# A fused model kernel: two sums of the recurrence moved to ScalarE, weights loaded in an earlier block, two layers cut into pieces

## The reference

```
x = x + mamba(rnn(x))          # rnn: h = tanh(h @ Wh + x_t @ Wx + b), 128 steps
                               # mamba: h = dA*h + dB*u, y = h.C ; y*rsqrt(mean(y^2)+eps)*norm_w*silu(z) @ out_proj
x = x + ffn(gru(x))            # gru: 128 steps; ffn: 3 residual blocks
                               #   h = h + qlora(gelu(layernorm(qlora(h))))
x = x + gla(cond_logits(x))    # gated linear attention
x = x + moe(lstm(x))           # lstm: 128 steps; moe: 8 experts, top 2
```

```python
y = y * lax.rsqrt(jnp.mean(jnp.square(y), axis=-1, keepdims=True) + eps) * norm_w
y = y * _silu(z)
return jnp.einsum('btd,od->bto', y, out_proj_w)
...
y = _qlora_linear(h, qweights[i0], scales[i0], biases[i0], lora_a[i0], lora_b[i0])
y = _layernorm(y, ln_gamma[blk], ln_beta[blk])
y = jax.nn.gelu(y, approximate=False)
y = _qlora_linear(y, qweights[i1], scales[i1], biases[i1], lora_a[i1], lora_b[i1])
h = y + h
```

## Time and profile before

| | us |
|---|---|
| median of 3 runs | 6985.24 (6977.26 to 6986.25) |
| the profiled execution | 6983.42 |
| its span, first to last instruction | 6981.6 |
| PE busy | 5730.2 (82%) |
| DVE busy | 5765.9 (83%) |
| ACT busy | 4481.1 (64%) |
| POOL busy | 2712.0 (39%) |
| between 2000 and 3000 us, in the recurrence: DVE, ACT busy | 917.1, 840.7 |
| between 5742 and 5797 us, in the finish: DVE, ACT busy | 37.6, 3.6 |
| between 6126 and 6160 us, in ffn: DVE, ACT busy | 19.9, 8.8 |

### The profile page before, as it was taken

One profiled execution on the slowest core, in us unless ns is written; L12 is line 12 of the kernel. 1 busy time (PEld: TensorE's weight loads), 2 busy tenths in 40 slices (PEclk: granted clock), 3 DMA queues, 4 the chain that ended last, 5 costly groups with the idle time before them and its releaser, 6 DMA issues. The chain is left out here.

```text
span 6981.6 us, 152684 instructions
## 1 busy us (share of the span) xinstructions
PE 5730.2 (82%) x49639; PEld 3105.1 (44%) x49913; DVE 5765.9 (83%) x11628; ACT 4481.1 (64%) x9795; POOL 2712.0 (39%) x2035
## 2 busy tenths in 40 slices
PE   5888888888888888888888768888888887934989
PEld 3555555555555555555555323333333334522543
DVE  4898999999999999989999789999999994446333
ACT  6888888888888888888888744444444442323322
POOL 3222222222222222222222179999999980000000
PEclk9999999999999999999999889999999998966999
DMA  0000000000000000000000010000000000000000
GB/s 8 2 2 2 2 2 2 2 2 2 2 2 2 2 2 2 2 2 2 2 2 2 20 31 4 4 3 4 4 3 4 4 2 3 4 7 3 0 18 6
DMA packets 14195, 30.48 MB, mean 4 GB/s; under 512 B 3665, under 2 KB 11602, under 8 KB 12434
## 3 DMA queue, kind: packets, MB, share of 16 engines
q1 hardware_dynamic: 13586, 22.47, 1.2%
HBM read 15.12 MB, written 7.34 MB: 3 GB/s over the span
## 5 line engine op out<-in xcount | busy, mean ns | idle before, releaser
L423 ACT ACTIVATE rx_junk<-rx_z 128x384 bf16<-128x384 f32 x2178 | 1371.5, 636 | 0.3
L1079 POOL TENSOR_TENSOR hc<-hh,cg 128x512 f32<-128x512 f32 x1024 | 1277.0, 1267 | 80.8 <-DVE hh L1059 75.3
L1000 ACT ACTIVATE ps_m<-ps_m,aneg 128x508 f32<-128x508 f32 x1024 | 673.6, 658 | 875.9 <-DVE hh L1059 834.3
L1059 DVE TENSOR_TENSOR_SCAN hh<-ps_m,bx 128x512 f32<-128x512 f32 x1024 | 1214.0, 1209 | 13.8 <-POOL bx L1083 13.8
L511 POOL TENSOR_TENSOR rx_z<-rx_z 128x512 f32<-128x512 f32 x256 | 384.8, 1503 | 1950.0 <-ACT rh_z L441 1946.7
L964 PE MATMUL ps_m<-hc,pick 128*128 128x512 f32 x2048 | 1056.0, 599 | 9.8 <-POOL hc L1079 8.5
L648 DVE TENSOR_REDUCE rh_ends<-rh_z 128x4 f32<-128x1536 f32 x512 | 960.3, 1917 | 124.3 <-ACT rh_z L441 124.3
L517 POOL TENSOR_TENSOR rx_z<-rx_z 128x1024 f32<-128x1024 f32 x274 | 656.0, 2395 | 73.4 <-DVE rx_z L612 36.7
L338 PE MATMUL r_ps<-rx_z,negid 128*128 128x256 f32 x2192 | 530.8, 384 | 103.2 <-POOL rx_z L511 90.6
L314 PE MATMUL r_ps<-rh_z,negid 128*128 128x256 f32 x2048 | 498.5, 385 | 111.6 <-ACT r_ps L435 111.6
L342 PE MATMUL r_ps<-rx_z,negid 128*128 128x512 f32 x1096 | 506.7, 605 | 62.2 <-POOL rx_z L517 62.2
(11 more groups left out here) (393 smaller groups left out, 10662.1 us busy)
## 6 DMA issues: line engine op xcount, KB each, us to landing
rows_scratch<-pc SPq DMA_DIRECT2D x48, 128.0 KB
rows<-rows_scratch SPq DMA_DIRECT2D x128, 48.0 KB
ew<-in_e SPq DMA_DIRECT2D x3, 1024.0 KB, 7.6
rh_z<-in_x_dn SPq DMA_DIRECT2D x1, 1024.0 KB, 4.8
xcur<-in_x_dn SPq DMA_DIRECT2D x1, 1024.0 KB, 5.3
out_x<-xcur SPq DMA_DIRECT2D x1, 1024.0 KB, 3.9
...
```

The source lines that it names most:

```text
L423: e.activation(junk[:, n % JUNK], xz[i][:, :, n, 2:K2].rearrange("p c k -> p k c"), ACT.Copy, accum_out=xsum[:, i, n:n + 1]).then_inc(x_fo ...
L1000: e.activation(da[un % NDA][:, :, 1:T], ps[:, un % 2, :].rearrange("p (n t) -> p n t", n=NG4)[:, :, 1:T], ACT.Exp, scale=aneg[:, 0:1]).the ...
L1059: e.tensor_tensor_scan(hh[un % NBUF][:], da[un % NDA].rearrange("p n t -> p (n t)"), bx[un % NBUF][:], 0.0, ALU.mult, ALU.add).then_inc(sc ...
L1079: e.tensor_tensor(hc[un % NHC][:], hh[un % NBUF][:], cg[:], ALU.mult).then_inc(weighted, 1)
```

## The change

1. **rnn.** The sums of the last two sequences (14 and 15) leave DVE: its fourth reduce covers two sequences instead of four, and ACT sums the two with an instruction of the same form as `x_fold`, behind the last `rest`. The sixteen x_fold of a step are distributed anew over the places of the step (before: 2, 1, 8, 5; now, with one place more: 2, 2, 1, 4, 7). POOL's `x_even_sums` no longer waits for ACT's `rest`, only for both DVE scans of x.
2. **The finish** of the state-space layer is done in four groups of four sequences; squares are made on ACT, the scale and eps of the mean are taken into the square root.
3. **Weights** of ffn, gla, lstm and moe get tiles that live from gru on, and their 24 transfers are issued in gru's block behind its own five. The copy of h stands first in ffn.
4. **ffn** works on two halves of the rows, each with its own counters; the engines take the halves in turn.

```diff
-        FIRST, SECOND, THIRD = 2, 3, 11
+        FIRST, GAP, SECOND, THIRD = 2, 4, 5, 9
...
                     seed(t, 1)
+                    x_fold(g - 1, other, FIRST, GAP)
                     e.wait_ge(re_mm, 2 * t + 1)
                     for c in range(2):
                         rest(c)
                     signs(1)
                     nudges(1)
-                    x_fold(g - 1, other, FIRST, SECOND)
+                    x_fold(g - 1, other, GAP, SECOND)
                     e.wait_ge(re_mm, 2 * t + 2)
                     for c in range(2, NRC):
                         rest(c)
+                    e.wait_ge(ra, KA * t + A_REST[NRC - 1])
+                    for i_ in range(TAIL):
+                        n = N - TAIL + i_
+                        e.activation(rjunk[:, i_], hz[:, :, n, 2:K2].rearrange("p c k -> p k c"), ACT.Copy,
+                                     accum_out=ends[:, n:n + 1]).then_inc(tail, 1)
...
+                    e.wait_ge(x_summed, 2 * g + 2)
                     for c in range(2):
-                        e.wait_ge(ra, KA * t + A_REST[2 * c])
                         x_even_sums(g, (s + 1) % 2, c)
                         x_negdifference(g, (s + 1) % 2, c)
...
                     for c in range(NRC):
                         e.wait_ge(ra, KA * t + A_REST[c])
-                        j = tl.inc(e.tensor_reduce(ends[:, quarter(c)], fold(hz, quarter(c)), mybir.AxisListType.XY, ALU.add))
+                        n = slice(quarter(c).start, min(quarter(c).stop, N - TAIL))
+                        j = tl.inc(e.tensor_reduce(ends[:, n], fold(hz, n), mybir.AxisListType.XY, ALU.add))
                     tl.wait(j)
+                    e.wait_ge(tail, TAIL * t + TAIL)
                     if s == 0:
                         e.wait_ge(xw_cp, i + 1)
                     j = tl.inc(e.tensor_tensor(pre[:], ends[:], xwT[:, s, :], ALU.add))
...
+                    for g in range(G):
+                        for h in range(H2):
+                            e.scalar_tensor_tensor(out=four(yz[:, g, h]), in0=four(yh[:, g, h]), scalar=nw[:, h:h + 1],
+                                                   in1=group(sz[:, h, :], g), op0=ALU.mult, op1=ALU.mult).then_inc(gated, 1)
...
+                    def add(g):
+                        e.wait_ge(projected, g + 1)
+                        e.tensor_tensor(group(xcur[:], g), group(xcur[:], g), four(ps[:, 4 + g, :]), ALU.add).then_inc(added, 1)
+
+                    for g in range(G):
+                        e.wait_ge(rooted, g + 1)
+                        e.reciprocal(rs[:, g], rs[:, g]).then_inc(inverted, 1)
+                        e.wait_ge(inverted, g + 1)
+                        e.wait_ge(gated, H2 * (g + 1))
+                        e.tensor_tensor(yz[:, g], yz[:, g], rs[:, g].unsqueeze(1).to_broadcast([128, H2, NG4 * T]),
+                                        ALU.mult).then_inc(scaled, 1)
+                        if g:
+                            add(g - 1)
+                    add(G - 1)
...
+                        e.activation(sq[:, g], yh[:, g], ACT.Square).then_inc(squared, 1)
+                    e.wait_ge(ready, 2)
+                    for g in range(G):
+                        e.wait_ge(total, g + 1)
+                        e.activation(rs[:, g], ps[:, g, :], ACT.Sqrt, scale=1.0 / DI, bias=eps[:, 0:1]).then_inc(rooted, 1)
...
+def load_later_weights(e, w, later):
+    tiles, loaded = later
+    f, a, l, x = (tiles[stage] for stage in "fale")
+    for dst, src in ((f["qi"][:], w["f_q"]), (f["sc"][:], w["f_s"]), (f["la"][:], w["f_la"]), (f["lb"][:], w["f_lb"]), (f["bias"][:], w["f_bc"])):
+        e.dma_start(dst, src).then_inc(loaded["f"], 16)
...
+    for dst, src in ((x["wr"][:], w["e_r"]), (x["w1"][:], w["e_1"]), (x["w3"][:], w["e_3"]), (x["w2"][:], w["e_2"])):
+        e.dma_start(dst, src).then_inc(loaded["e"], 16)
...
+                load_later_weights(e, w, later)
...
+                def rise(b, hf):
+                    if b == 0:
+                        e.wait_ge(made, V0)
+                    else:
+                        e.wait_ge(vec[hf], b * KV)
+                    for c in CHUNKS(hf):
                         for k in range(4):
                             j = e.matmul(ps[:, c, k * D:(k + 1) * D], h[:, (4 * c + k) * 128:(4 * c + k + 1) * 128],
                                          wt[:, 2 * b, :], start=True, stop=True)
-                        j.then_inc(pe, 1)
-                    for c in range(4):
-                        e.wait_ge(act, b * KA + 3 + c)
+                        j.then_inc(pe[hf], 1)
+
+                def fall(b, hf):
+                    for i, c in enumerate(CHUNKS(hf)):
+                        e.wait_ge(act[hf], b * KA + 3 + i)
                         for k in range(4):
                             j = e.transpose(ps[:, 4 + c, k * D:(k + 1) * D], y[:, 4 * c + k, :], ident[:])
-                        j.then_inc(pe, 1)
-                    for c in range(4):
-                        e.wait_ge(act, b * KA + KA)
+                        j.then_inc(pe[hf], 1)
+                    e.wait_ge(act[hf], b * KA + KA)
+                    for c in CHUNKS(hf):
                         e.matmul(ps[:, c, :], wt[:, 2 * b + 1, :], yT[:, c * 512:(c + 1) * 512], start=True, stop=True)\
-                            .then_inc(pe, 1)
+                            .then_inc(pe[hf], 1)
+
+                rise(0, 0)
+                rise(0, 1)
+                for b in range(3):
+                    fall(b, 0)
+                    if b < 2:
+                        rise(b + 1, 0)
+                    fall(b, 1)
+                    if b < 2:
+                        rise(b + 1, 1)
...
+                    for hf in range(2):
+                        e.wait_ge(vec[hf], b * KV + 4)
+                        e.activation(sq[:, rows8(hf), :], yc[:, rows8(hf), :], ACT.Square).then_inc(act[hf], 1)
+                        e.wait_ge(vec[hf], b * KV + 6)
+                        e.activation(rs[:, rows8(hf)], rs[:, rows8(hf)], ACT.Sqrt).then_inc(act[hf], 1)
+                        e.wait_ge(vec[hf], b * KV + 10)
+                        for c in CHUNKS(hf):
+                            e.activation(y[:, 4 * c:4 * c + 4, :], yc[:, 4 * c:4 * c + 4, :], ACT.Gelu).then_inc(act[hf], 1)
+                        e.wait_ge(pe[hf], b * KPE + 4)
+                        e.activation(yT[:, cols(hf)], ps[:, 4 + 2 * hf:6 + 2 * hf, :].rearrange("p a b -> p (a b)"),
+                                     ACT.Copy).then_inc(act[hf], 1)
...
+                s.inc(e.tensor_copy(h[:], XF))
                 e.wait_ge(loaded, 16 * 8)
...
+                def norm(b, hf):
+                    s, r = track[hf], rows8(hf)
+                    bc = lambda x, k: x[:, b, :].unsqueeze(1).to_broadcast([128, k, D])
+                    per = lambda x: x[:, r].unsqueeze(2).to_broadcast([128, 8, D])
+                    for i, c in enumerate(CHUNKS(hf)):
+                        e.wait_ge(pe[hf], b * KPE + i + 1)
+                        s.inc(e.tensor_tensor(yc[:, 4 * c:4 * c + 4, :], ps[:, c, :].rearrange("p (k d) -> p k d", k=4), bc(brow, 4), ALU.add))
                     s.sync()
+                    s.inc(e.tensor_reduce(mu[:, r], yc[:, r, :], AXX, ALU.add))
                     s.sync()
+                    s.inc(e.scalar_tensor_tensor(out=yc[:, r, :], in0=per(mu), scalar=-1.0 / D, in1=yc[:, r, :], op0=ALU.mult, op1=ALU.add))
+                    e.wait_ge(act[hf], b * KA + 1)
+                    s.inc(e.tensor_reduce(rs[:, r], sq[:, r, :], AXX, ALU.add))
                     s.sync()
+                    s.inc(e.tensor_scalar(rs[:, r], rs[:, r], 1.0 / D, 1e-5, ALU.mult, ALU.add))
+                    e.wait_ge(act[hf], b * KA + 2)
+                    s.inc(e.reciprocal(mu[:, r], rs[:, r]))
                     s.sync()
+                    s.inc(e.tensor_tensor(yc[:, r, :], yc[:, r, :], per(mu), ALU.mult))
                     s.sync()
+                    s.inc(e.tensor_tensor(yc[:, r, :], yc[:, r, :], bc(gam, 8), ALU.mult))
                     s.sync()
+                    s.inc(e.tensor_tensor(yc[:, r, :], yc[:, r, :], bc(bet, 8), ALU.add))
+
+                def residual(b, hf):
+                    s = track[hf]
+                    for i, c in enumerate(CHUNKS(hf)):
+                        e.wait_ge(pe[hf], b * KPE + 5 + i)
                         hc = h[:, c * 512:(c + 1) * 512]
                         s.inc(e.scalar_tensor_tensor(out=hc, in0=ps[:, c, :], scalar=bias[:, 2 * b + 1:2 * b + 2], in1=hc,
                                                      op0=ALU.add, op1=ALU.add))
                     s.sync()
+
+                for b in range(3):
+                    norm(b, 0)
+                    if b:
+                        residual(b - 1, 1)
+                    norm(b, 1)
+                    residual(b, 0)
+                residual(2, 1)
+                for hf in range(2):
```

(23 more changed lines are left out.)

183 lines of the change are left out of this document (68 added, 115 removed).

## The result

The changed kernel takes **6889.77 us** (median of 4 runs, 6885.62 to 6891.72) against 6985.74 for the kernel before on the same chip: ratio 0.9864, 95% interval 0.9848 to 0.9880. That is 1.4% faster, 96 us, where 169 were forecast (6816, range 6788 to 6866). Each part of the change does what it was built for and the sign is right; more than two thirds of the biggest term is missing.

The account below looks back on a forecast made before the run. The prediction saw a chain in every stage, not a full engine, as the bound. Recurrence 106, finish 20, loads 28, warm start 3 and halves 12 sum to 169 us off, 6816 us, own range 6793 to 6838, overall 6788 to 6866.

Parts of the forecast that it names:

- The recurrence: Recurrence loop: each of 128 steps 0.83 us shorter, 106 us in all, bounds 70 to 118.
- The shortened reduce: Recurrence step: DVE's fourth reduce covers two sequences instead of four and saves 0.87 us a step.
- holder of the product of h: Recurrence step: x_copy allows L289 at 2023.15, DVE's tanh chain wants it at 2023.46, a cover of 0.3 us.
- The new wait of `pre` for `tail`: Recurrence step: ACT's new sums end about 2012.0, the shortened reduce at 2012.95, so this wait costs nothing.
- Rival A: Recurrence: L289 waits for x_copy, the step gains 0.5 us, 64 us instead of 106; 6858 us, chance 0.12.
- B: Recurrence: the shortened reduce saves nothing in the loop, only the 63 us outside remain; 6922 us, chance 0.04.
- C: Recurrence: ACT becomes the bound at the first rest, 92 us lost, 63 gained outside; 7014 us, chance 0.04.
- D: gru: the change works but gru's start suffers 5 us from the transfers; inside the forecast's own range.
- The finish: End of the state-space layer: work in four groups, squares on ACT, saves 20 us, bounds 17 and 22.
- The loads: Starts of ffn, gla, lstm and moe: weights loaded early end the waits for DMA, 28 us saved.
- the warm start: Later blocks: PE's filler keeps it awake, so their first matmuls run at its faster clock; 3 us, 0 to 9.
- The halves: Feed-forward layer on two halves of the rows: 12 us saved, bounds 5 and 16.

Follow-up runs that it names:

- pool_late: Changed kernel, but POOL again waits for the first rest before its even sums, as before the change: 6952.54 us, ratio 0.9954 to the kernel before.
- no_fillers: Changed kernel with one fold moved behind x_copy, POOL released sooner, and no filler matmuls (useless ones that keep PE busy): 6999.67 us, ratio 1.0020 to the kernel before.
- fold_early: Changed kernel with one more x_fold behind x_copy, leaving six instead of seven behind the copies for tanh: 6840.60 us, ratio 0.9789 to the kernel before.
- before_five: Kernel before the change with five filler matmuls a step instead of ten, nothing else changed: 6958.14 us, ratio 0.9966 to the kernel before.
- five_fillers: Changed kernel with five filler matmuls a step instead of ten: 6836.63 us, ratio 0.9794 to the kernel before.
- warm_ffn_more: Changed kernel with one fold moved, five fillers, POOL sooner, and 5, 11, 11, 11 useless matmuls in the feed-forward layer: 6774.18 us, ratio 0.9700 to the kernel before.

## Why the prediction was wrong

**The recurrence (106 forecast, 30 measured).** The shortened reduce is worth what it was sized at: 0.89 a step in the trace for 0.87. Three steps behind it failed: a wait of `pre` for POOL that was put at nothing, a wait in ScalarE's queue that was left out, and the wrong holder of the product of h.

1. "The new wait of `pre` for `tail` therefore costs nothing, with 0.9 us to spare." That wait does cost nothing, but `pre` has another cover that was not looked for: it is not over before POOL's last sum is (8.28 behind 8.25, 8.86 behind 8.82, 8.87 behind 8.83). pool_late moves POOL by 0.57 and `pre`, h and the step move by 0.57 or 0.58 with it. `pre` ends 0.58 earlier where the reduces end 0.89 earlier: 0.3 a step, 38 us. The sign was in the earlier trace rows: `pre` at 2013.85 lasts 0.38 for 16 columns, where h's instruction of the same shape lasts 0.17, and it ends at 2014.23, where L342, released by POOL, begins at 2014.25. The Trainium skill has the rule, in "SBUF — State Buffer", section "Who interferes with whom": a VectorE instruction with two inputs in SBUF and a GpSimd instruction that reads SBUF share a port pair, it is held for the whole instruction, and the one that comes second waits. The trace agrees in both directions (`pre` 1.18 us behind POOL, POOL 2.28 behind the scan), and so it does with the same section's remark that a reduce does not contend: in no_fillers, where POOL is early, the shortened reduce takes 1.02 with POOL at work and without, and the others 1.92 either way.
2. "2010.5 + 0.1 + 1.25 + 2.5 + 0.7 + 4.4 = 2019.5, where L415 then starts." The sum went through ScalarE's queue as if nothing in it waited. But the copies for tanh wait for DVE, L491 for the square of x and L496 for L181, and before L496 ScalarE stands 0.31: from L491 to the next fold it is 1.17 (2026.15 to 2027.32), not 0.7. So x_rest_copy is 5.96 us behind DVE's square, with seven folds in between. That is 14.49, 0.43 after PE's result, which came when it was forecast to; the sum had the two in step. Moving one fold ahead gave 0.39 of it back (fold_early, 49 us).
3. "So L289 is allowed at 2019.5 + 1.77 + 1.88 = 2023.15", by x_copy. Neither x_copy nor DVE held it but PE's own queue: the fillers wait for x_rest_copy, take 2.1 us and stand in front. The term of the sum for L289 should have read x_rest_copy's end + 2.4. So it was before the change, too: "By the tanh chain, 0.87 earlier, it is wanted at 2023.46" took for granted that DVE's chain held L289 in the earlier trace rows, and before_five shows 0.4 us of fillers between h and it. five_fillers shows the same in the changed kernel: the product of h 0.58 earlier, everything up to h unchanged.

Rival A (6858) had the right kind of cause, ScalarE's chain of x in the place of DVE's, and the wrong link; even its least gain of 0.4 a step was too much by the fillers. B and C did not happen: the reduces became as short as sized, and from the product of h to the next first rest it is 9.89 us (median) where it was 9.90, though ScalarE has no idle time left before the first rest. D did not happen either: gru was not slower for 24 more transfers.

**The finish** (20 forecast, 20.1): right, step by step. **The loads** (28 and 3 for the warm start; first add of the feed-forward layer 7.6, gla, lstm and moe 23.9 together, 31.5 in all): the waits are right one by one; in gla, lstm and moe they gave 21.5 of the 23.9, where 21.2 were forecast. The warm start is there (moe's first matmuls take 3.71 instead of 7.00, lstm's 32 take 13.97 instead of 16.29), but moe does not keep it: from its first matmul to the output's transfer it is 249.3 where 248.9 stood. Between 6713 and 6753 us the granted clock is 0.91, and it was 1.00 in the like stretch before (6808 to 6848). What lowers it there is open.

**The halves** (12 forecast, 7.6 measured): the mis-sized term is the norm of a half. It was sized at 10.9 with 1.33 to 2.17 before it; in the last two blocks it has 2.23 or 2.24 before it each time and 0.78 to 0.95 between its two adds (6108.16 and 6109.80), because PE comes to the map at its lower clock; a half takes 15.2 (from the first add at 6108.16 to the next half's at 6123.37) where 13.9 to 14.8 stood. warm_ffn_more shows it: with a short pause before the map a half takes 13.5. The feared late Sqrt did not come: twelve table loads of 1.28 are all covered.
